# A two-layer block (cross-attention, then a mixture of experts): gates at the gather, another order in the turn, x joined in the product, a mask for an expert's number

## What is computed

```python
x = x + xattn(layernorm(x), ctx, Wq, bq, Wkv, bkv, Wo, bo)     # 16 heads of 16, a bias by distance of query and key, softmax
x = x + moe(layernorm(x), Wg, bg, W1, b1, W2, b2)

def moe(x, ...):
    gate = softmax(x @ Wg + bg)                  # 8 experts
    top, idx = top_k(gate, 2)
    top = top / (sum(top) + 1e-08)
    # for each of the two experts e of a row, weighted by top:
    y = gelu(x @ W1[e] + b1[e]) @ W2[e] + b2[e]  # 256 -> 1024 -> 256
```

## Time and profile before

| | |
|---|---|
| median of three runs | 441.41 us |
| profiled execution | 444.43 us, span 442.6 us |
| TensorE (PE) busy | 398.0 us, 90% |
| VectorE (DVE) busy | 317.0 us, 72% |
| ScalarE (ACT) busy | 221.5 us, 50% |
| GpSimd (POOL) busy | 201.2 us, 45% |
| chain that ended last | PE 60%, DVE 15%, DMA 9%, issue 6% |
| TensorE clock granted, mean | 0.974 |

### The profile page before, as it was taken

The page is one execution under the profiler, slowest core; times in us unless marked ns, Lnnn a source line. Parts: engine busy times, 40 slices in busy tenths (PEclk is TensorE's granted clock), DMA queues, the critical chain, the costliest instruction groups (busy, mean ns, idle before and its releaser), DMA issues.

```text
span 442.6 us, 15274 instructions
## 1 busy us (share of the span) xinstructions
PE 398.0 (90%) x4882; PEld 309.7 (70%) x4882; DVE 317.0 (72%) x872; ACT 221.5 (50%) x587; POOL 201.2 (45%) x337
## 2 busy tenths in 40 slices
PE   5878898888899999889999999999999999999960
PEld 3756676666677877678777777777777777777740
DVE  6576898888898886682578778766666666666660
ACT  2335777677776654463567444443444444444420
POOL 3301378777777865564357222333223222232241
PEclk9988999999999999998999999999999999999995
DMA  7557687677777664235434474333322233333210
GB/s 271 124 139 242 190 272 236 190 195 226 200 204 215 194 170 127 93 111 87 143 62 64 62 137 61 49 49 51 50 44 40 42 43 46 43 49 47 27 14 0
DMA packets 75218, 51.02 MB, mean 115 GB/s; under 512 B 50560, under 2 KB 69120, under 8 KB 75008
## 3 DMA queue, kind: packets, MB, share of 16 engines
q1 hardware_dynamic: 67944, 41.57, 36.4%
q0 software_dynamic: 7152, 8.47, 11.2%
q10 hardware_dynamic: 48, 0.01, 0.0%
HBM read 28.59 MB, written 17.50 MB: 104 GB/s over the span
## 4 chain that ended last, share of the span: by engine, by line
PE 60%; DVE 15%; DMA 9%; issue 6%; POOL 3%; SPq 2%; ACT 2%; ACTq 0%; DVEq 0%; POOLq 0%
PE ps L1191 57%; DMA out<-stage,row_id 4%; DVE wts L885 4%; DVE mx L900 3%; DMA area<-in_x 2%; PE ps L1320 1%; PE ps L1326 1%; DMA md<-nbT 1%; DVE xn L830 1%; DVE st L820 1%; DMA area<-qd 1%; POOL rs L544 1%; POOL rs L548 1%; ACT wts L655 1%; ACT area L791 1%
## 5 line engine op out<-in xcount | busy, mean ns | idle before, releaser
L1191 PEld LDWEIGHTS ps<-stage,wts 128*128 x1872 | 131.3, 98 | 44.0 <-issue 6.3
L1191 PE MATMUL ps<-stage,wts 128*128 128x128 f16 x1872 | 158.9, 220 | 0.6 <-issue 0.5
L1191 PE MATMUL ps<-wts,area 128*128 x624 | 151.2, 327 | 0.3 <-DVE area L1118 0.2
L791 ACT ACTIVATE area<-ps,late 128x128 f32<-128x128 f32 x312 | 89.2, 370 | 116.8 <-PE ps L1191 116.7
L620 POOL DMA_INDIRECT out<-stage,row_id x39 | 65.1, 1669 | 135.0 <-DVE stage L1143 77.2
L1116 DVE TENSOR_SCALAR area<-area 128x512 f16<-128x512 f32 x78 | 33.9, 435 | 57.1 <-ACT area L791 55.5
L1191 PE MATMUL ps<-area 128*128 128x128 f16 (+3 forms) x832 | 68.3, 236 | 4.3 <-DVE mx L900 2.1
L1191 PEld LDWEIGHTS ps<-area 128*128 128x128 f16 (+1 forms) x832 | 51.6, 104 | 14.2 <-issue 4.8
L661 ACT ACTIVATE area<-ps 128x512 f32<-128x512 f32 x80 | 47.1, 598 | 28.5 <-PE ps L1191 28.0
L1118 DVE SCALAR_TENSOR_TENSOR area<-area 128x512 f16<-128x512 f32 x78 | 55.1, 706 | 2.7
L900 DVE TENSOR_REDUCE mx<-ps 128x3 f32<-128x462 f32 (+1 forms) x96 | 53.1, 575 | 3.1 <-PE ps L1191 2.9
(11 more groups left out here) (132 smaller groups left out, 408.8 us busy)
## 6 DMA issues: line engine op xcount, KB each, us to landing
stage<-in_w SPq DMA_DIRECT2D x32, 512.0 KB, 4.1
area<-qd SPq DMA_DIRECT2D x16, 256.0 KB
qd<-wts SPq DMA_DIRECT2D x48, 64.0 KB, 3.0
area<-in_x SPq DMA_DIRECT2D x16, 128.0 KB, 5.4
out<-area SPq DMA_DIRECT2D x16, 128.0 KB
xlist<-pad_rows SPq DMA_DIRECT2D x15, 130.0 KB
area<-in_b SPq DMA_DIRECT2D x1, 1024.0 KB, 5.9
area<-in_kink SPq DMA_DIRECT2D x1, 944.0 KB
```

The costliest lines, as they stand in the source:

```text
L791: last = nc.scalar.activation(h32[par][:, c * P:(c + 1) * P], h_ps[par][m][:, f * P:(f + 1) * P], ACT.Gelu_apprx_tanh, bias=b1T[:, ds(e[t] ...
L1191: return nc.tensor.matmul(out_, lhsT, rhs, start=start, stop=stop, skip_group_check=skip)
```

## The change

- `weights_of` becomes `tail_of`: GpSimd writes the row's number, the first expert and the raw exponential of the second; ScalarE's `routing_exp` writes their sum straight into `rows`. The gate weight is worked out at the gather, in `extract` on VectorE (three instructions become six, one of them a reciprocal).
- GpSimd's turn puts `rstd1` ahead of `least` and `chosen`, and `rows_lo` behind them.
- VectorE's turn is ordered anew (in the diff); the first of the two splits is that of a unit of the turn before.
- `output_product` begins with a product of the identity and the tile of x, so that PSUM holds the sum; ScalarE's new `residual_out` copies it into `xr` and signals x2_d. L930 is gone. For the last tile it stands at k = 2 on ScalarE, and VectorE's `residual` moves from k = 1 to k = 2.
- Five numbers to a word instead of eight; TensorE masks a number where it stands in the word, and the stride of the address makes up for the place. ScalarE and VectorE shift and mask where they use it.

```diff
@@ -23,7 +23,7 @@
-WORDS = 3
+FIVE, WORDS = 5, 5
...
@@ -332,13 +332,16 @@
             _, words_ = nc.values_load_multi_w_load_instructions(sched_i[0:1, 1, WORDS * phase:WORDS * (phase + 1)], engines=[eng.engine],
-                                                                 min_val=0, max_val=E ** E - 1,
-                                                                 skip_runtime_bounds_check_because="eight numbers of no more than E - 1")
-            return [(words_[k // E] >> (3 * (k % E))) & (E - 1) for k in range((K1, NBLK - K1)[phase])]
+                                                                 min_val=0, max_val=E ** FIVE - 1,
+                                                                 skip_runtime_bounds_check_because="five numbers of no more than E - 1")
+            return [(words_[k // FIVE], k % FIVE) for k in range((K1, NBLK - K1)[phase])]
+
+        def number(place):
+            return (place[0] >> (3 * place[1])) & (E - 1)
         def expert_at(t):
-            return t if t < K1 else WORDS * E + t - K1
+            return t if t < K1 else WORDS * FIVE + t - K1
...
@@ -567,22 +570,14 @@
-            def weights_of(t, q):
+            def tail_of(t, q):
+
                 words_ = rows[:, q, 2 * D:ROW]
-                z, zsum = e8[:, 1:2], small[:, 1:2]
                 pool.tensor_copy(words_[:, 0:2].bitcast(i32), ids[:, t:t + 1]).then_inc(s.tail_d, 1)
-                pool.wait_ge(s.e8_d, t + 1)
-                pool.tensor_scalar(small[:, 2:3], zsum, 1e-8, 1.0, ALU.mult, ALU.add).then_inc(s.gates, 1)
                 pool.wait_ge(s.mi_d, t + 1)
                 pool.tensor_copy(words_[:, 2:4].bitcast(f32), mi[:, 0:1]).then_inc(s.tail_d, 1)
-                pool.wait_ge(s.gates, 4 * t + 1)
-                pool.tensor_tensor(small[:, 3:4], small[:, 2:3], z, ALU.add).then_inc(s.gates, 1)
-                pool.wait_ge(s.gates, 4 * t + 2)
-                pool.tensor_tensor(small[:, 4:5], small[:, 3:4], c32[:, C_MINUS:C_MINUS + 1], ALU.pow).then_inc(s.gates, 1)
-                pool.wait_ge(s.gates, 4 * t + 3)
-                pool.tensor_tensor(words_[:, 6:8].bitcast(f32), small[:, 4:5], z, ALU.mult).then_inc(s.gates, 1)
-                pool.wait_ge(s.gates, 4 * t + 4)
-                pool.tensor_tensor(words_[:, 4:6].bitcast(f32), small[:, 4:5], words_[:, 6:8].bitcast(f32), ALU.subtract).then_inc(s.tail_d, 1)
+                pool.wait_ge(s.e8_d, t + 1)
+                pool.tensor_copy(words_[:, 4:6].bitcast(f32), e8[:, 1:2]).then_inc(s.tail_d, 1)
...
@@ -601,14 +596,13 @@
                     dispatch(b2 - 1, (b2 - 1) % 2)
-                if b2 is not None:
-                    rows_lo(b2, b2 % 2)
-                    least(b2)
-                    chosen(b2)
                 if f1 is not None:
                     rstd1(f1)
                 if b2 is not None:
-                    weights_of(b2, b2 % 2)
+                    least(b2)
+                    chosen(b2)
+                    rows_lo(b2, b2 % 2)
+                    tail_of(b2, b2 % 2)
...
@@ -701,6 +695,8 @@
                 if mt is not None:
                     exps(mt, 3)
                     exps(mt, 4)
+                if b1 is not None:
+                    residual_out(b1)
                 if f1 is not None:
                     normed1(f1)
                 for u in units[1:2]:
...
@@ -724,10 +720,16 @@
+            def residual_out(t):
+                act.wait_ge(s.pr_ps, t + 1)
+                nc.scalar.copy(xr[:, t % 8, :], misc[:, D:2 * D]).then_inc(s.x2_d, 1)
+
             def routing_exp(t):
                 act.wait_ge(s.nm_d, t + 1)
                 wait(act, s.tail_d, 3 * t)
-                nc.scalar.activation(e8[:], m8[:], ACT.Exp, bias=small[:, 0:1], accum_out=small[:, 1:2]).then_inc(s.e8_d, 1)
+                wait(act, S[f"scat{t % 2}"], 32 * (t // 2))
+                nc.scalar.activation(e8[:], m8[:], ACT.Exp, bias=small[:, 0:1], 
+                                     accum_out=rows[:, t % 2, ROW - 2:ROW].bitcast(f32)).then_inc(s.e8_d, 1)
...
@@ -789,7 +791,7 @@
                     last = nc.scalar.activation(h32[par][:, c * P:(c + 1) * P], h_ps[par][m][:, f * P:(f + 1) * P],
-                                                ACT.Gelu_apprx_tanh, bias=b1T[:, ds(e[t] * FC + c, 1)], scale=1.0 / (SX * SW))
+                                                ACT.Gelu_apprx_tanh, bias=b1T[:, ds(number(e[t]) * FC + c, 1)], scale=1.0 / (SX * SW))
...
@@ -803,6 +805,8 @@
                 gelu_half(k, e)
+                if k == 2:
+                    residual_out(NT - 1)
...
@@ -926,9 +930,8 @@
             def residual(t):
-                dve.wait_ge(s.pr_ps, t + 1)
-                dve.tensor_tensor(xr[:, t % 8, :], misc[:, D:2 * D], xr[:, t % 8, :], ALU.add).then_inc(s.x2_d, 1)
                 dve.wait_ge(s.x2_d, t + 1)
+                wait(dve, s.mv2_d, t)
...
@@ -1025,20 +1028,22 @@
             def turn(i):
                 f1, f2, sc, mt, b1, b2 = stages(i)
-                units, earlier = weight_units(i), weight_units(i - 1)
+                earlier = weight_units(i - 1)
                 if b2 is not None and b2 > 0:
                     positions(b2 - 1)
+                if b2 is not None:
+                    normed2(b2)
+
+                for u in earlier[0:1] if i < NT - 1 else earlier[1:2]:
+                    split_w_lo(u)
+                if f1 is not None:
+                    norm1(f1)
                 if sc is not None:
                     maxima(sc, 0)
-                    maxima(sc, 1)
-                if b2 is not None:
-                    normed2(b2)
-                if sc is not None:
-                    maxima(sc, 2)
                 if f2 is not None and f2 > 0:
                     query_lo(f2)
-                if i == NT - 1:
-                    split_w_lo(earlier[1])
+                if sc is not None:
+                    maxima(sc, 1)
...
@@ -1048,22 +1053,19 @@
                     first_schedule()
                 if sc is not None:
+                    maxima(sc, 2)
                     maxima(sc, 3)
-                if f1 is not None:
-                    norm1(f1)
                 for u in earlier[1:2] if i < NT - 1 else []:
                     split_w_lo(u)
+                if i == NT - 2:
+                    split_w_lo(weight_units(i)[0])
                 if sc is not None:
                     maxima(sc, 4)
-                for u in units[0:1]:
-                    split_w_lo(u)
                 if b1 is not None:
                     residual(b1)
+                    aggregated(b1)
                 if sc is not None:
                     maxima(sc, 5)
-                if b1 is not None:
-                    aggregated(b1)
-                if sc is not None:
...
@@ -1122,12 +1124,20 @@
                 wait(dve, s.y_done, t - 3)
-                dve.scalar_tensor_tensor(out=wsel[:, slot, 0:1], in0=pay[slot][:, 1:2], scalar=sched_f[:, 1, expert_at(t):expert_at(t) + 1],
-                                         in1=pay[slot][:, 2:3], op0=ALU.is_equal, op1=ALU.mult).then_inc(s.wa_d, 1)
+                first, z, zsum = (pay[slot][:, n:n + 1] for n in (1, 2, 3))
+                dve.tensor_scalar(wsel[:, slot, 0:1], zsum, 1e-8, 1.0, ALU.mult, ALU.add).then_inc(s.wa_d, 1)
+
+                dve.scalar_tensor_tensor(out=wsel[:, slot, 3:4], in0=first, scalar=sched_f[:, 1, expert_at(t):expert_at(t) + 1], in1=z,
+                                         op0=ALU.is_equal, op1=ALU.max).then_inc(s.we_d, 1)
+                dve.wait_ge(s.wa_d, t + 1)
+                dve.tensor_tensor(wsel[:, slot, 1:2], wsel[:, slot, 0:1], z, ALU.add).then_inc(s.wc_d, 1)
                 wait(dve, s.added, 16 * (t - 3))
                 dve.tensor_copy(row_id[:, slot:slot + 1], pay[slot][:, 0:1].bitcast(i32)).then_inc(s.wb_d, 1)
-                dve.wait_ge(s.wa_d, t + 1)
-                dve.tensor_tensor(wsel[:, slot, 1:2], wsel[:, slot, 0:1], pay[slot][:, 3:4], ALU.add).then_inc(s.ex_d, 1)
+                dve.wait_ge(s.wc_d, t + 1)
+                dve.reciprocal(wsel[:, slot, 2:3], wsel[:, slot, 1:2]).then_inc(s.wd_d, 1)
+                dve.wait_ge(s.wd_d, t + 1)
+                dve.wait_ge(s.we_d, t + 1)
+                dve.tensor_tensor(wsel[:, slot, 0:1], wsel[:, slot, 2:3], wsel[:, slot, 3:4], ALU.mult).then_inc(s.ex_d, 1)
...
@@ -1140,7 +1150,7 @@
-                dve.tensor_scalar(ysb[par], ysb[par], wsel[:, t % 4, 1:2], None, ALU.mult).then_inc(s.y_done, 1)
...
@@ -1152,7 +1162,7 @@
                     extract(k // 2)
-                if k == 1:
+                if k == 2:
...
@@ -1345,8 +1355,10 @@
                     pe.wait_ge(s.c16_in, 32)
+
+                mm(misc[:, D:2 * D], ident, xr[:, t % 8, :], True, False)
                 for c in range(DC):
-                    mm(misc[:, D:2 * D], oT[:, c * P:(c + 1) * P], wos[:, c, :], c == 0, False)
+                    mm(misc[:, D:2 * D], oT[:, c * P:(c + 1) * P], wos[:, c, :], False, False)
```

(19 more changed lines are left out.)

21 lines of the change are left out of this document (11 added, 10 removed).

## The result

| | before | after |
|---|---|---|
| median on one chip | 441.87 us (441.26 to 445.16, 4 runs) | 453.78 us (452.97 to 455.34, 4 runs) |
| profiled execution | 444.43 us, span 442.6 | 455.34 us, span 453.5 |
| TensorE clock granted, mean | 0.974 | 0.966 |

The ratio is 1.0258, 95% interval 1.0199 to 1.0318: slower, as forecast, but by 11.9 us instead of 6.1, and 0.8 us above the top of the range (453). Lines moved: the logits are L918 (were L914), the residual's statistics L935 (L932), norm1 L824 (L820), maxima L904 (L900), exps L655 (L661), output_back L1349 (L1339), the helper of the products L1201 (L1191). L725 is now ScalarE's new copy of the sum.

The account below looks back on a forecast made before the run. The bound was taken to be a loop through in-order queues (normed2, transpose, logits, VectorE's queue). Terms 5.0 + 3.2 + 0.6 + 0.9 + 0.5 - 4.1 = +6.1 us on 441.41 gave 447.5 us, range 440.5 to 453 (8 in 10).

Parts of the forecast that it names:

- at 11.1 they take 77.7: +3.2 us: Turns 3 to 9: all seven turns last 11.1 us, 77.7 us together against 74.5, so +3.2 us.
- The loop: VectorE's way from logits to logits: 5.2 us to x2_d plus 5.9 back, 11.1 us a turn against 10.74.
- The start: Up to the logits of turn 2: norm1 ahead of the maxima moves them from 55.75 to 60.7, +5.0 us (+3 to +7).
- rival two: Steady turns: the load of x for norm1 becomes the loop; median landing adds 0.5 us a turn, 451 us; chance 0.17.
- Turns 10 to 15: Late turns: six identity products add 3.3 us, less waits given back, 1.04 us twice and some 0.6: +0.6 us.
- Before the experts: Turn 15: the copy comes behind exps 4, so normed2 starts at 208.1 instead of 207.2, +0.9 us.
- The expert part: Expert blocks: TensorE keeps only the mask, 33 blocks save 0.125 us each, -4.1 us (-3 to -4.6).
- An early copy: Steady turns: ScalarE's copy ends early enough, so TensorE bounds the turn at 10.2 us; 441.2 us in all; chance 0.2.
- rival three: Expert blocks: the mask doesn't pay, the 4.1 us stay, 451.6 us; chance 0.08.

Follow-up runs that it names:

- the dummy products: Changed kernel plus 16 unread products of 128 columns in TensorE's gap ahead of output_back, for tiles 2 to 10: 449.45 us.
- the last kernel of set C: Changed kernel with norm1 behind the maxima in turns 0 and 1, ScalarE's copy before its last exponential, maxima 5 and negation before the second statistics: 444.24 us.
- the chip of set B: Four runs sharing a chip where the kernel before took 438.18 us; the changed kernel unaltered took 454.29 us there, ratio 1.0371.

## Why the prediction was wrong in size

Profiled against profiled, the span grew by 10.9 us:

| stretch | forecast | measured | from |
|---|---|---|---|
| to the logits of turn 2 | +5.0 | +4.0 | 55.75 to 59.74 |
| turns 3 to 9 | +3.2 | +10.5 | 74.5 to 84.9 |
| turns 10 to 15, before the experts | +0.6, +0.9 | -1.2, -0.2 | expert part begins 13.1 later |
| expert part, with the last tile | -3.6 | -2.2 | the rest |

**The failed step** is "at 11.1 they take 77.7: +3.2 us". The 11.1 was right (10.87, or +1.6 for seven turns). What failed is that all seven would be such turns. Turns 4, 6 and 8, with the lower clock, took 2.89, 1.56 and 1.57 us more than 10.87: **6.0 us are in the half-clock turns**. Turns 3, 5 and 7, in which norm1 waited 1.51, 0.65 and 0.41 us for its load, took 1.60, 0.74 and 0.49 us more: 2.8. With 1.6 for the loop that is the 10.5. The sum had nothing for the clock, because I had read TensorE's idle time in a turn only as room, and the load only as a rival. The 9 us that two of the expectations put on the stretches was too much.

With the dummy products the seven turns took 78.9 us (58.87 to 137.81), 6.0 less than 84.9: 4.5 of it in turns 4, 6 and 8, 1.5 in the others. Two more profiled executions of the changed kernel took 82.7 and 85.2 us, so the gain is 4 to 6 us. The Trainium skill (TensorE: Matmul & The Clock Gate, Part 1) describes two clock states set by how busy TensorE has been; the windows at 0.50 and 1.00 agree with the two states.

**The loop** was right part by part. VectorE's wait for the copy was 1.10 us instead of 1.5 to 2, because its long split grew from 1.19 us to 1.68 in this turn. The prediction's point that ScalarE's queue leaves the copy no place ahead of exps 4 held, and moving it there gave 6.8 us. The identity product took 0.54 us from start to start (135.67 to 136.21), as taken from the earlier trace rows; the estimate from the Trainium skill (FP8 and Floating Point Precision, TensorE Precision Notes), 0.43 us, is too low here. The prediction's own range, 444.5 to 450.5, is not what its bounds give: 447.5 with 2.0 and 0.5 less, and with 2.0 and 1.1 more, is 445.0 to 450.6.

**The start** was right in place, and 1 us too dear. **The x load** (rival two) was never the loop, but norm1 waited for it in turns 3, 5 and 7, by 2.6 us together, near the 3.5 us that the rival had at the median landing.

**Turns 10 to 15:** the term was 1.8 us too high. The waits given back were worth more than the 2.7 us I counted: 3.3 of new products and a net of -1.2 make 4.5. I had 0.6 us for all smaller waits; VectorE's waits at the logits of these six turns alone were 0.40 to 0.88 us each and 3.8 together before, and 0.32 in all after. On another chip there was less to give back: the mask alone, whose attention part is that of the kernel before, took 66.4 us for these turns in its trace, against 68.5 before and 67.3 after.

**Before the experts:** +0.9 was forecast and -0.2 came. normed2 of tile 14 started at 220.27 where I had it at 221.4 (207.2, 13.3 for what came before, 0.9). The kernel before was at half clock from 198.0 to 201.4 in the profiled execution, inside this stretch, and the changed one was not; that made the term look better than it is.

**The expert part:** a block lost 0.11 us in the last twenty (109.86 to 107.59), forecast 0.125, inside its bounds. The sum is smaller because seven of the first blocks, with the last tile's work among them, won nothing (40.67 us before, 41.10 after) and because TensorE stops longer where it loads the second schedule's words. Timeline of TensorE, kernel before, then after:

```profile
303.26 0.65 PE L1191 MATMUL ps<-stage,wts 128*128 128x128 f16 x6 [0.53 <-issue]
```
```profile
316.24 0.64 PE L1201 MATMUL ps<-stage,wts 128*128 128x128 f16 x6 [0.99 <-issue]
```

That is +0.46 us for five words instead of three, where I allowed 0.1 to 0.3.

**The rivals.** An early copy exists, but only after an edit: the copy first gave 10.26 us, the rival's 10.2. The mask pays, so rival three fails.

**Still open:** what makes the clock fall. The stop of 1.28 us stands in the full-clock turns too, and turns of the last kernel of set C kept full clock with stops of 0.99 to 1.29 us. In the three profiled executions of the changed kernel norm1 waited for its load eight times in turns 3 to 9 (0.30 to 1.51 us), and each time the clock fell 1.5 to 3.7 us later; one more fall came without such a wait. It isn't a rule: in the last kernel of set C a wait of 0.47 us was followed by none. No kernel was run that takes away these waits and nothing else, so which of the stops the clock answers to is not shown. Also open is why the kernel before takes 437 us on some chips and 441 to 443 on others while the changed one stays at 454. Its trace is from one chip only, where turns 5 to 8 take 10.7 to 10.8 us and VectorE waits some 0.8 us at the logits; the mask alone on another chip has 10.20 and 0.17 there. In all three profiles of the changed kernel VectorE doesn't wait at the logits in turns 3 to 9. That may be why the change costs 12 us here and 16 on the chip of set B, but no run shows it.

## What to carry to other kernels

When the bound is a loop through in-order queues, an engine's freed work is worth nothing until the instruction that closes the loop moves forward in its own queue: here one swap on ScalarE gave back 6.8 of the 16 us that the bundle had lost on that chip. When you change the order of one engine, follow what the others wait for: GpSimd's new order with VectorE's old one gave turns of 11.82 us. An instruction that takes a load stands badly at the front of a queue: its waits come ahead of all the rest. Test the parts of a bundle singly: mask and gates alone were faster, the bundle was slower. Where a busy TensorE will stand still longer, look at the granted clock by turn, not only at its mean.
